# A first attention in which VectorE adds a third of the logarithms that TensorE added

## What is computed

```
scores = jnp.einsum('bhqd,bhkd->bhqk', q, k) * scaling
scores = scores + _power_law_mask(S, scores.dtype)[None, None]   # -log(delta + 1), -inf for delta < 0
attn = jax.nn.softmax(scores, axis=-1)
out = jnp.einsum('bhqk,bhkd->bhqd', attn, v)
out = out.transpose(0, 2, 1, 3).reshape(B, S, D)
out = out @ w_proj + b_proj
```

## Time and profile before

| | us |
|---|---|
| median of 3 runs | 1056.6 (1056.46 to 1058.58) |
| the profiled execution | 1050.06 |
| its span | 1048.3 |
| TensorE busy | 888.4 (85%) |
| VectorE busy | 636.2 (61%) |
| GpSimd busy | 519.9 (50%) |
| ScalarE busy | 464.0 (44%) |

### The profile page before, as it was taken

How to read it: one execution, slowest core, us unless ns; L and a number is a source line. 1 busy time by engine, 2 the same in 40 slices (tenths; PEclk the granted TensorE clock), 3 DMA queues, 4 the chain that set the end, 5 groups by cost and what they waited for, 6 DMA issues and landing times. The chain is left out here.

```text
span 1048.3 us, 18106 instructions
## 1 busy us (share of the span) xinstructions
PE 888.4 (85%) x6388; PEld 606.9 (58%) x6388; DVE 636.2 (61%) x1768; ACT 464.0 (44%) x1119; POOL 519.9 (50%) x504
## 2 busy tenths in 40 slices
PE   5689899999999986668998999986999994599992
PEld 3123333333334574645666889985886674488982
DVE  5887787778782466675886557782006566543334
ACT  5235565666557634261114747764433221132220
POOL 3646988898898733632233335654100001266651
PEclk9658999999999999686997889997999997699997
DMA  6800111011000000010000000302000000376664
GB/s 192 254 1 2 32 32 31 2 32 32 3 1 3 1 17 8 16 42 1 2 2 1 22 12 21 139 2 81 1 1 1 1 21 21 120 218 210 209 216 131
DMA packets 38751, 55.78 MB, mean 53 GB/s; under 512 B 7066, under 2 KB 26146, under 8 KB 38534
## 3 DMA queue, kind: packets, MB, share of 16 engines
q1 hardware_dynamic: 36154, 49.50, 16.0%
q0 software_dynamic: 2496, 5.12, 1.7%
q10 hardware_dynamic: 12, 0.01, 0.0%
HBM read 43.47 MB, written 10.94 MB: 52 GB/s over the span
## 5 line engine op out<-in xcount | busy, mean ns | idle before, releaser
L515 POOL TENSOR_TENSOR arena<-arena 128x1024 f32<-128x1024 f32 (+3 forms) x100 | 195.4, 1991 | 30.6 <-ACT arena L714 30.6
L799 DVE CUSTOM_DVE_ANT_0 ps<-ps,arena 128x512 f32<-128x512 f32 (+3 forms) x256 | 148.8, 641 | 39.7 <-PE ps L581 39.0
L714 ACT ACTIVATE arena<-ps 128x512 f32<-128x512 f32 (+3 forms) x320 | 137.2, 490 | 79.4 <-PE ps L612 51.4
L581 PE MATMUL ps<-arena 48*128 48x512 bf16 (+3 forms) x384 | 103.8, 367 | 25.6 <-DVE arena L799 13.4
L156 POOL TENSOR_SCALAR vareps<-meanvar 128x4 f32<-128x4 f32 x32 | 8.2, 256 | 173.8 <-DVE meanvar L103 172.6
L581 PEld LDWEIGHTS ps<-arena 48*128 48x128 bf16 x384 | 28.3, 95 | 92.2 <-DVE arena L799 52.4
L2280 PE MATMUL ps<-arena 128*128 128x128 f32 x624 | 77.4, 278 | 0.0
L2280 PEld LDWEIGHTS ps<-arena 128*128 128x128 f32 x624 | 74.0, 195 | 0.0
L604 PE MATMUL ps<-arena 51*128 51x512 bf16 (+3 forms) x384 | 73.5, 341 | 0.6 <-ACT arena L727 0.2
L633 PE MATMUL ps<-arena 128*9 128x512 f32 (+3 forms) x640 | 66.1, 488 | 0.6 <-POOL arena L515 0.4
L515 POOL TENSOR_TENSOR xnT<-xnT,arena 128x1024 f32<-128x1024 f32 (+1 forms) x28 | 52.6, 1899 | 27.1 <-ACT xnT L714 27.1
(11 more groups left out here) (349 smaller groups left out, 2063.0 us busy)
## 6 DMA issues: line engine op xcount, KB each, us to landing
arena<-in_L_ffn_w SPq DMA_DIRECT2D x39, 512.0 KB, 3.9
arena<-scratch SPq DMA_DIRECT2D x32, 192.0 KB, 4.0
arena<-in_L_ffn_w SPq DMA_DIRECT2D x16, 256.0 KB, 3.7
scratch<-arena SPq DMA_DIRECT2D x12, 256.0 KB, 3.0
arena<-expert_rows SPq DMA_DIRECT2D x8, 256.0 KB, 4.8
scratch<-arena SPq DMA_DIRECT2D x4, 384.0 KB, 3.2
scratch<-arena SPq DMA_DIRECT2D x12, 128.0 KB, 2.9
x<-in_x SPq DMA_DIRECT2D x4, 256.0 KB, 4.4
```

The costliest lines, as they stand in the source:

```text
L515: nc.gpsimd.tensor_tensor(e, e, weight[:, at:at + k].unsqueeze(1).broadcast_to([P, 2, k]), ALU.mult).then_inc(weighed, 1)
L581: nc.tensor.matmul(m.ps[:, (2 * k + e) % MAX_BANKS, 0:wd], qs[rows, u % BUFS, pair, i * P:(i + 1) * P], ks[rows, u % BUFS, pair, first:fir ...
L714: nc.scalar.activation(probs(g)[:, 2 * p + e, 0:wd], m.ps[:, BANK[h, e], 0:wd], ACT.Exp, scale=SCALE).then_inc(exps, 1)
L799: nc.vector.tensor_tensor_reduce(out=scores, in0=scores, in1=before[:, 0:wd], scale=-1.0, scalar=negrest[:, h, i:i + 1] if i < TPC else 3e ...
```

## The change

Of the 64 halves that are not GpSimd's, 21 are put in `BY_VECTOR`: every fifth, and all of the last unit. For these the four matmuls of L611 and L612 are left out. `add_log` on VectorE waits for the scores (`s_mm`) and adds the table in float32 in place, in PSUM, one add for each of the half's two banks, and ScalarE's exponential waits for its semaphore `logged` instead of `s_mm`. In VectorE's order `add_log` stands where `schedule` has the half's `exp`. The tiles for the turned outputs, `oT`, take `masked` first and then `logw`, since `logw` is now read until the end of the last unit.

```
@@ -272,7 +272,7 @@
-    oT = [a[:, n * CH:(n + 1) * CH] for a in (logw, masked) for n in range(S // CH)]
+    oT = [a[:, n * CH:(n + 1) * CH] for a in (masked, logw) for n in range(S // CH)]
@@ -375,6 +376,9 @@
     BY_POOL = shares()
+    LOG = [h for h in range(UNITS * HALVES) if h not in BY_POOL]
+
+    BY_VECTOR = [h for n, h in enumerate(LOG) if h >= (UNITS - 1) * HALVES or n % 5 == 4]
@@ -596,7 +600,7 @@
-            with_log = h not in BY_POOL
+            with_log = h not in BY_POOL and h not in BY_VECTOR
@@ -710,7 +714,10 @@
             for e in range(2):
-                act.wait_ge(s_mm, 2 * h + e + 1)
+                if h in BY_VECTOR:
+                    act.wait_ge(logged, 2 * BY_VECTOR.index(h) + e + 1)
+                else:
+                    act.wait_ge(s_mm, 2 * h + e + 1)
@@ -800,6 +807,15 @@
+        def add_log(u, at):
+            n, p = at
+            h, wd, off = u * HALVES + 2 * n + p, width(n), weight_at(n)
+            for e in range(2 if h in BY_VECTOR else 0):
+                dve.wait_ge(log_steps, 5)
+                dve.wait_ge(s_mm, 2 * h + e + 1)
+                scores = m.ps[:, BANK[h, e], 0:wd]
+                nc.vector.tensor_tensor(scores, scores, logw[:, off:off + wd], ALU.add).then_inc(logged, 1)
@@ -833,7 +849,7 @@
-        do = {"max": maximum, "split": split_maxima, "divide": divide, "add": add, "normalise": lambda _, c: following.normalise(dve, c)}
+        do = {"max": maximum, "exp": add_log, "split": split_maxima, "divide": divide, "add": add, "normalise": lambda _, c: following.normalise(dve, c)}
```

More of the change, by code:

```diff
@@ L297, in l0_attn @@
     log_steps = sem("l0a_log_steps")
+    logged = sem("l0a_logged")
     pv_mm, num_out, num_turned, rec_set, o_set = (sem(f"l0a_{n}") for n in ("pv_mm", "num_out", "num_turned", "rec_set", "o_set"))
@@ L847, in l0_attn @@
                 (num_turned, QC * UNITS), (rec_set, QC * UNITS), (o_set, QC * UNITS), (o_turned, NC), (oT_set, NC), (y_mm, NC), (v_ones, 2),
-                (cleared, 1), (nsplit, 3 * UNITS), (tails_in, 16 * 2 * BUFS), (log_steps, 7)]
+                (cleared, 1), (logged, 2 * len(BY_VECTOR)), (nsplit, 3 * UNITS), (tails_in, 16 * 2 * BUFS), (log_steps, 7)]
     m.spent += [(stack_in[n], STACK * len(range(n, UNITS, BUFS))) for n in range(BUFS)]
```

## The result

| | before | after |
|---|---|---|
| median of 20 runs each | 1056.81 us (1049.23 to 1062.35) | 1063.3 us (1058.98 to 1071.73) |
| ratio, 95% interval | | 1.0061 [1.0041, 1.008] |
| profiled execution, span | 1048.3 us | 1061.4 us |
| start of half 24 to start of half 168 (units 1 to 6) | 218.42 | 223.29 |
| start of half 168 to the end of the attention | 33.03 | 40.60 |

The kernel became 6.5 us slower; the forecast was 1062.5. The two profiled executions cannot be subtracted as they stand: before's, with 1050.1 us, is nearly as short as the fastest of its 20 runs, and after's, with 1063.23, lies at its median. So I read them stretch by stretch. First the page of after: the granted clock in 40 slices, and TensorE's group of the scores with its idle time (last figures: idle before them, releaser).

The account below looks back on a forecast made before the run. TensorE was taken to bound the attention by little (33.9 of a unit's 36.4 us), with VectorE in a loop. Terms -0.5 (units 0 to 6) + 3.9 (stall) + 2.5 (clock) = 5.9 us on 1056.6 gave 1062.5, range 1060.8 to 1065.5.

Parts of the forecast that it names:

- The order: Last unit, VectorE: eight normalising instructions, the second four slowed by GpSimd's weighing, end at 347.65 ahead of half 178's adds.
- The size of the stall: Last unit: waiting behind the normalising moves the attention's end from 359.45 to 363.3, 3.9 us lost despite 9.4 of matmuls removed.
- The walk: Last unit, followed instruction by instruction at full clock: TensorE stands still from about 342.3 to 348.8 and ends at 363.3.
- The clock: Last unit, TensorE: the 6.5 us idle gap brings half speed from about 346 to 360, adding 2.5 us.
- Up to half 177 nothing changes: Start of the last unit: adds of 172, 173 and 176 end when their logarithm matmuls would have.
- The additions: VectorE, two PSUM adds per half: one takes 0.69 us at 512 columns, 0.55, 0.43 and 0.30 at 384, 256 and 128.
- The rival that GpSimd blocks them too: VectorE's adds wait for GpSimd's weighing as the normalising does; 20 us more, 1080 us; chance 0.04.
- Units 0 to 6: Ten halves moved to VectorE: counted place by place, about 0.5 us won of 7.8 us of matmuls removed.
- No stall: Last unit: GpSimd yields to the waiting normalising, adds hide, GpSimd's end at 357.4 bounds; 1055.6 us, no change; chance 0.11.
- pays in full: Units 0 to 6: TensorE bounds every unit, so removal wins 7.8 us; 1052.7 with stall, 1048.3 without; chance 0.08.
- The stall without a fall: Last unit: TensorE stalls behind the normalising but its clock stays full; 1060.0 us; chance 0.18.
- Half clock into the next part: Last unit and beyond: the stall comes and half clock lasts past the attention, 8.5 us for the clock; 1068.5 us; chance 0.11.

Follow-up runs that it names:

- e9: e5 with the useless products in place of removed matmuls only up to half 179, the 28 before half 180 kept; ratio 1.0024.
- e2: The kernel before with only the last unit's eleven halves given to VectorE, units 0 to 6 as before; 1065.19 us, ratio 1.0064.
- e3: The changed kernel with the eight normalising instructions (L110) moved behind half 191's additions; 1055.83 us, ratio 0.9981.
- e4: e2 with the eight normalising instructions (L110) moved behind half 191's additions; 1057.02 us, ratio 0.9976.
- e8: e4 with GpSimd weighing only the last unit's even halves up to 186 and VectorE adding for the other fourteen; 1057.24 us, ratio 1.0024.
- e5: e2 plus useless TensorE products: four for each of the eleven halves and 28 just before half 180; ratio 1.0077.
- e6: e4 plus four useless TensorE products for each of the last unit's eleven VectorE halves, as many as were removed; ratio 0.9997.
- e12: e11 plus twelve halves of units 0 to 6, where e1 gained, moved to VectorE; 1064.35 us, ratio 0.9996 to the kernel before.
- e1: The kernel before with only the ten halves of units 0 to 6 given to VectorE, last unit as before; 1056.9 us, ratio 1.0.
- e7: The kernel before with the eight normalising instructions (L110) moved behind half 191, no additions moved; ratio 0.9991.
- e11: e8 plus two useless TensorE products for each of the last unit's VectorE halves; ratio 0.9994.
- e10: e8 plus useless TensorE products for VectorE's halves, four each up to half 177 and two each after; ratio 0.9977.

## Why the prediction was right, step by step

**The order.** Predicted: L110 from 339.25 to 347.65, 12.8 to 21.2 us after half 168. At full clock (e9) 12.95 to 21.33. In after 14.11 to 22.14: the clock's first fall made half 176's scores late, and then the first four were the slow ones (7.0 us) and the second four the quick ones, since GpSimd's run of weighings had already begun (344.92 against 345.22) and ended (351.88) before them. The sum was nearly the same, 8.03 us against the 8.4 predicted.

**Who waits.** The next addition at once: yes, 353.17. ScalarE 7 us: 6.90. TensorE 6.5 us before half 180: 5.86. GpSimd's end at 361.35, 34.9 us after half 168: 34.9 in e9 (369.52 - 334.62), 36.7 in after.

**The size of the stall.** 3.9 us predicted (the attention's end 36.9 us after half 168), 2.2 to 3.5 from e9. The walk was long by 0.4 to 1.7 us.

**The clock.** 2.5 us predicted, 4.1 to 5.4 by the estimate above: this term of the sum was the mis-sized one, and it was the larger of the two, not the smaller. The total for the unit, 6.4 predicted and 7.6 measured, hides that the stall was too large in it and the clock too small. That the forecast came as near as 0.8 us is in part luck: the two errors have opposite signs. I had placed one stretch of half clock from about 346 to 360, after the gap. In after there were three. The one behind the gap (352.0 to 358.8) was shorter than I said. The one ahead of it (338.3) broke the step "Up to half 177 nothing changes": it put half 180 at 23.26 instead of the 22.4 of the walk. The third lay on the last four products and cost 2.1 us there alone.

Behind it stands a step of the prediction: I had tied a fall to an idle gap, as the three places of the earlier trace rows suggested, and as the Trainium skill ("TensorE: Matmul & The Clock Gate", Part 1) has it for an idle array. The runs show that a gap is not needed, and so does a fall further on in the trace of before, which the prediction left out (windows up to it and from it):

```profile
599.30:606.30 7.00, 6.67 (x51) 6.06 (x49) 4.88 (x14) 4.68 (x20) 4.28 (x8) 1.00 0.01 2
606.30:616.50 10.20, 8.80 (x33) 7.90 (x34) 3.29 (x5) 1.53 (x4) 2.00 (x5) 0.50 0.08 26
```

All five kernels with the additions in the last unit and no useless products (after, e2, e3, e4, e8) have a fall 6.5 to 7.2 us after half 168. TensorE had no idle stretch over 0.2 us since half 168 in four of them, and none over 1 us in e8. Of the six with useless products (e5, e6, e9 to e12) none has one there, nor have before and e1, which keep the logarithm matmuls. e7, which keeps them too, had one at 10.3 us, of 3.4 us, behind an idle stretch of 1.21 us that before has at the same place without a fall. So the removal itself goes with the first fall, as far as fourteen executions, one each and e7 between the groups, can show it. Busy time alone does not part them. The first 6.54 us of the last unit, e2's up to its fall and e11's, which has none:

```profile
326.56:333.10 6.54, 6.07 (x46) 2.25 (x45) 5.64 (x22) 5.21 (x10) 4.90 (x3) 1.00 0.00 1
328.82:335.36 6.54, 5.86 (x39) 2.36 (x38) 6.16 (x22) 3.79 (x8) 3.69 (x2) 1.00 0.01 1
```

Why the clock fell in one and not in the other stays open.

**The additions.** Two of 512 columns took 1.30 us, of 384 1.02, of 256 0.76, of 128 0.50 (predicted 1.38, 1.10, 0.86, 0.60), with GpSimd busy beside most of them. The rival that GpSimd blocks them too (1080 us) is out. The Trainium skill ("SBUF — State Buffer", "Who interferes with whom") parts the two kinds of instruction in the same way, and the runs agree: 0.65 us for an addition of 512 columns, 2.4 for a normalising one of 128.

**Units 0 to 6.** Predicted 0.5 won; e1 lost 0.4 from half 24 to half 168, and won 0.4 at half 14. The sum is near, but not by its terms. Gain by place, predicted and measured (e1 against before, by the start of each half):

| half | 14 | 34 | 47 | 63 | 80 | 93 | 114 | 131 | 143 | 159 |
|---|---|---|---|---|---|---|---|---|---|---|
| predicted | -0.3 | 0.75 | 0.4 | -0.15 | -0.1 | -0.4 | 0.3 | -0.1 | 0.4 | -0.35 |
| measured | 0.43 | 0.17 | 0.15 | 0 | 0.05 | -0.24 | -0.10 | -0.27 | 0.15 | -0.26 |

The sign is wrong at 14, 80 and 114. At 34, 47 and 143 VectorE's idle time was there, and only 0.15 to 0.17 came of it; what took the rest wasn't tried. At 80 0.19 us was won and 0.14 lost by half 88, at 114 0.47 won and 0.57 lost by half 118, and at 131 0.28 won and 0.55 lost by half 136. That 7.8 us of removed matmuls bring nothing is firm: the three units of after that had no fall (the second, fifth and sixth) took 36.11, 36.27 and 36.21 us, where before took 36.44, 35.75 and 36.38.

**Two sums of the prediction** do not come out as they stand, and neither moved the forecast. The bound of 3 us lost in units 0 to 6 is given as 8.5 less the idle time at 34, 47 and 143, but 8.5 less 1.16 and twice 1.20 is 4.9. And 11.2 us at half speed (348.8 to 360) are 5.6 us of work, not 6, which gives 365.1 for the end and not 364.9.

**After's 223.29 us.** 4.9 us of the difference between the two profiled executions lie in units 1 to 6. They aren't the change's: e1 has its additions there and 218.83, e7 and e4 have none of them and 225.0. They are falls of the clock that come by execution: e4, e5 and e7 to e11 had some there too. The medians of 20 runs average over them, and their difference of 6.5 us fits the 7.6 of the last unit and e1's 0 within the intervals ([4.3, 8.5] us for after, by the ratio).

**The rivals.** "No stall" and "pays in full" fell with the 8.03 us. "The stall without a fall" came in no run without stand-in work. Half clock into the next part (1068.5) came in part: after had it from 365.6 to 372.4, 0.7 us beyond the end of the attention, and again at 382.7. The second is not the stall's doing alone, since e7, e10 and e11, without a stall, have a fall of the same 3.4 us at 377.2, 377.4 and 369.8.

## What to carry to other kernels

Before giving an engine a step that others wait for, read its queue for instructions that were slow and harmless until then: an 8.81 us entry on an idle engine is a stall as soon as something waits behind it, and moving it by some places is worth more than the work shifted. Removed work pays only up to the next bound, here GpSimd's 31 us of weighing. And work taken from TensorE can come back as clock, which together with the stall cost more here than the stall by itself (4.1 to 5.4 us against 2.2 to 3.5) and at most 0.9 us without it (e3 and e4 beside e6); where GpSimd has less to do, two useless products per half were cheaper than the falls (31.41 us in e11 against 33.35 in e8).

## What the runs showed of the hardware

- TensorE's granted clock falls at other places from one execution of the same code to the next. Ten executions with units 1 to 6 of the kernel before took 218.42, 218.76, 218.77, 221.57, 222.18, 223.93, 225.04, 225.06, 225.07 and 228.22 us for them. These 9.8 us compare with a spread of 13.1 us in before's 20 runs (1049.23 to 1062.35), and hide any gain of 1 to 2 us.
- A fall to half clock (1.2 GHz) does not need an idle engine: in after the one at 338.3 came with TensorE busy for 6.46 of the 7.19 us before it, in before the one at 606.3 for 6.67 of 7.00. Nor does busy time alone decide it: e2 fell after 6.07 busy of 6.54 us, e11 did not after 5.86 of 6.54. How it is decided stays open.
- Four normalising instructions on VectorE took 1.1 us where GpSimd had no weighing and 7.0 to 8.8 us where it had, whichever four they were.
